# Target attention on one core: the small projections of the TensorE loop moved from inside the context to between turning and scores

## The reference

```
q = (target_item @ W_q).reshape(b, 4, 32)
k = (history @ W_k).reshape(b, 200, 4, 32)
v = (history @ W_v).reshape(b, 200, 4, 32)
scores = einsum('bhd,bshd->bhs', q, k) / sqrt(32)
scores = where(mask[:, None, :] == 0, -1e9, scores)
attn = softmax(scores, axis=-1)
y = einsum('bhs,bshd->bhd', attn, v).reshape(b, 128) @ W_o
```

## Time and profile before

| what | value |
|---|---|
| median of 3 runs | 581.31 us (579.66 to 874.48) |
| the profiled execution's own time | 575.58 us |
| its span, first to last instruction | 573.6 us |
| what lies around the span | 2.0 us |
| TensorE busy | 97% of the span |
| VectorE busy | 87% |
| packets of the main DMA queue | 96.4% of 16 engines' span |
| moved | 219.06 MB, 382 GB/s over the span |

### The profile page before, as it was taken

How to read it: one execution, slowest core, us unless ns; L and a number is a source line. 1 busy time by engine, 2 the same in 40 slices (tenths; PEclk the granted TensorE clock), 3 DMA queues, 4 the chain that set the end, 5 groups by cost and what they waited for, 6 DMA issues and landing times.

```text
span 573.6 us, 41769 instructions
## 1 busy us (share of the span) xinstructions
PE 553.6 (97%) x18612; PEld 444.7 (78%) x18612; DVE 497.4 (87%) x577; ACT 298.7 (52%) x949; POOL 307.3 (54%) x1126
## 2 busy tenths in 40 slices
PE   5878999999999999999999999999999999999996
PEld 5656878778887878787887888888788778878785
DVE  4876889999998988999998999989999899989970
ACT  2334555555455555555546555554655555455453
POOL 6844365565555556456546555655654555565500
PEclk9999999999999999999999999999999999999999
DMA  8998999999999999999999999999999999999940
GB/s 312 411 360 313 363 407 394 408 408 406 400 412 405 399 408 381 409 405 412 406 403 408 404 405 406 411 398 404 405 406 406 393 410 396 406 408 396 408 173 7
DMA packets 66120, 219.06 MB, mean 382 GB/s; under 512 B 7616, under 2 KB 16464, under 8 KB 66080
## 3 DMA queue, kind: packets, MB, share of 16 engines
q1 hardware_dynamic: 64800, 217.31, 96.4%
q0 software_dynamic: 704, 1.05, 0.5%
q10 hardware_dynamic: 576, 0.30, 0.2%
HBM read 217.58 MB, written 1.05 MB: 381 GB/s over the span
## 4 chain that ended last, share of the span: by engine, by line
PE 89%; DVE 3%; issue 3%; DMA 2%; SPq 1%; ACT 0%; POOLq 0%; POOL 0%; DVEq 0%
PE ps_c L288 35%; PE ps_s L258 31%; PE ps_p L271 10%; PE ps_y L298 6%; PE ps_u L243 4%; PE ps_u L305 4%; DVE blocks L477 3%; DMA hist<-r_history_sequence 2%; SPq L155 1%; ACT p_pad L412 0%; SPq L146 0%; DVE probs_t L498 0%; DVE neg_score L486 0%; POOLq L46 0%; POOL out L229 0%
## 5 line engine op out<-in xcount | busy, mean ns | idle before, releaser
L477 DVE STREAM_TRANSPOSE blocks<-hist 128x768 f32<-128x768 f32 (+2 forms) x320 | 469.8, 1490 | 51.8 <-DMA hist<-r_history_sequence 51.5
L201 POOL COPY u_pad<-u_sb 32x32 f32<-32x32 f32 x1024 | 234.4, 229 | 63.1 <-ACT u_sb L391 3.9
L288 PE MATMUL ps_c<-hist,p_pad 64*32 64x128 f32 x12800 | 217.4, 272 | 5.4 <-issue 4.6
L288 PEld LDWEIGHTS ps_c<-hist,p_pad 64*32 64x32 f32 x12800 | 182.6, 105 | 33.4 <-issue 25.3
L258 PE MATMUL ps_s<-blocks,u_pad 128*32 128x200 f32 x4096 | 189.1, 334 | 3.2 <-issue 1.9
L412 ACT ACTIVATE p_pad<-ps_p,own 128x200 f32<-128x200 f32 x512 | 170.2, 444 | 34.2 <-PE ps_p L271 34.2
L258 PEld LDWEIGHTS ps_s<-blocks,u_pad 128*32 128x32 f32 x4096 | 125.5, 110 | 46.6 <-DVE blocks L477 4.7
L205 POOL TENSOR_SCALAR bias<-mask 128x200 f32<-128x200 int32 x64 | 56.4, 882 | 175.9 <-DMA mask<-r_mask 175.7
L421 ACT COPY ctx_sb<-ps_c 128x128 f32<-128x128 f32 x128 | 27.8, 269 | 101.1 <-PE ps_c L288 101.1
L395 ACT ACTIVATE probs<-neg_score,neg_max 128x200 f32<-128x200 f32 x64 | 29.6, 463 | 95.5 <-DVE neg_max L486 95.5
L271 PE MATMUL ps_p<-probs_t,place_sel 128*64 128x112 f32 x1024 | 63.2, 265 | 1.2 <-DVE probs_t L498 0.9
(11 more groups left out here) (42 smaller groups left out, 83.1 us busy)
## 6 DMA issues: line engine op xcount, KB each, us to landing
hist<-r_history_sequence SPq DMA_DIRECT2D x128, 832.0 KB, 7.6
hist<-r_history_sequence SPq DMA_DIRECT2D x128, 512.0 KB, 6.0
hist<-r_history_sequence SPq DMA_DIRECT2D x128, 256.0 KB, 4.5
mask<-r_mask SPq DMA_DIRECT2D x64, 100.0 KB, 7.9
out<-out_sb POOLq DMA_DIRECT2D x21, 48.0 KB, 5.3
x_t<-r_target_item SPq DMA_DIRECT2D x1, 928.0 KB, 16.7
x_t<-r_target_item ACTq DMA_DIRECT2D x1, 96.0 KB, 4.4
w_in<-L_rec_W_k ACTq DMA_DIRECT2D x1, 64.0 KB, 1.9
```

What stands on the lines that cost most here:

```text
L201: pool.tensor_copy(to, source[Q * c:Q * c + Q, a]).then_inc(u_pad_ready, 1)
L288: mm = pe.matmul(ps_c[alpha][at:at + Q, 0:D], p_pad[rows, t + par, i, :], hist[2 * ring + i][rows, t + par, :], start=(t == 0), stop=(t + ...
L477: dve.transpose(blocks[g % BLOCKS][:, t0:t1].rearrange("p t c k -> p (t c k)"), hist[g % SLOTS][:, t0:t1, :].rearrange("p t d -> p (t d)") ...
```

## The change

Two things move. In TensorE's step, the small projection leaves the context, whose three pieces now follow each other, and stands between `turn_context` and `scores`. The kinds are dealt out anew: ring 0 does heads 2 and 3 of the next round, ring 1 does the outputs, ring 2 does heads 0 and 1 of the round after. The start does only heads 0 and 1 of round 1. On ScalarE the copy of the combined vectors and the copy of the output go to the end of the step's list, behind the copy of the turned context.

```diff
@@ step (TensorE)
                 turn_context()
+                if ring == 0:
+                    combine(r + 1, (2, 3))
+                if ring == 1:
+                    outputs(q - 1)
+                if ring == 2:
+                    combine(r + 2, (0, 1))
                 scores(q + 1, after, 0)
                 scores(q + 1, after, 1, q + 1)
-                for piece in range(len(PIECES) - 1):
+                for piece in range(len(PIECES)):
                     context(ring, piece)
-                if ring == 0:
-                    outputs(q)
-                else:
-
-                    combine(r + 2, (2 * ring - 2, 2 * ring - 1))
-                context(ring, len(PIECES) - 1)
...
-            combine(1, range(H))
+            combine(1, (0, 1))
@@ copy_combined (ScalarE)
-                act.wait_ge(u_done, r + 1 if r < 2 else 2 * r)
+                act.wait_ge(u_done, 2 * r + 1)
@@ the loop of ScalarE
                 exponent(q)
                 normalise(q)
+                if q >= 1:
+                    finish(q - 1)
+                expand(q)
+                if q >= 1:
+                    copy_context(q - 1)
                 r = q // RING
                 if q % RING == 0 and r + 1 < NR:
                     copy_combined(r + 1)
                 if q % RING == 1 and r >= 1:
                     store(r - 1)
-                if q >= 1:
-                    finish(q - 1)
-                expand(q)
-                if q >= 1:
-                    copy_context(q - 1)
```

## The result

The changed kernel is **slower**: 586.54 us median (585.75 to 588.28, 5 runs) against 581.31 (5 runs), a ratio of 1.0119 with a 95% interval of 1.0085 to 1.0152, so +5 to +9 us; the two medians alone differ by 5.2. The ratio is taken over fast runs, so without the one of 874.48 us that stands among the runs of before. The profiled execution took 585.75 us, its span 583.7. I had forecast 580.6: wrong in sign. The measured time lies outside the forecast's own range of 572.3 to 584.2, and inside the range of eight in ten (571 to 588) only because that one made room for rival B.

The account below looks back on a forecast made before the run. TensorE and the DMA engines were taken as both full, balanced to about 2%. Start +2.5, steady part -2.2 and end -1.0 gave -0.7 us, forecast as a 580.6 us median; own range 572.3 to 584.2, eight in ten 571 to 588.

Parts of the forecast that it names:

- rival B: Start: the new wait for the target transfer is paid in full, no earlier loss saved; 591 to 593 us; chance 0.12.
- The start's term: First iteration: combine's new wait for the large target transfer costs +2.5 us, between +0.4 and +3.9.
- The stop of the loads: Start: loads stop from 32 until slots come free at 37.8 and about 1 us more; 6.8 us lost.
- The wait itself: Ring 0, first iteration: TensorE idles about 10 us, from 22.4 until the target transfer lands at 32.8.
- The clock behind it: Combine and scores behind the start's wait: cold matmuls add 0 to 3.3 us, taken as 1.
- The steady part and the end: From 110 to 545 us -2.2 us, a quarter of 8.4; after the last load -1.0 us.
- GpSimd at no cost: GpSimd's spread begins later in one step of three, but its reader comes some 9 us later; cost 0.
- VectorE's longer wait for history: Steady part: TensorE's gain becomes waiting behind VectorE, whose wait for history grows beyond 51.5 us.
- Rival A: Steady part: TensorE is the real bound and loads speed up to 412 to 420 GB/s; 571.4 to 566.4 us; chance 0.13.
- Rival C: Context's break costs nothing or its gain comes back, loads gain nothing; only the start's +1 to +4 remains; chance 0.15.
- half-way case: Start: the wait for the target transfer is paid in part, +5 us, 586 us.
- far end: Start: wait of 11.4 us plus 1 to 3.3 for cold matmuls, less 3 elsewhere: +9.4 to +11.7, 591 to 593 us.

Follow-up runs that it names:

- e2: Kernel before, nothing moved, but TensorE waits for the large target transfer in ring 0 ahead of the scores; ratio 1.0168 to the kernel before.
- e1: Changed kernel, but ring 0's combine doesn't wait for the large target transfer in the first iteration; 578.25 us, ratio 0.9951 to the kernel before.
- e7: Kernel before with the outputs doing one head of four, so less TensorE work; ratio 0.9943 to the kernel before.
- e14: Kernel before with each mask from pair 3 on loaded a second time into a tile nobody reads; ratio 1.0220 to the kernel before.
- e9: Kernel before with the masks of pairs 3 to 63 not loaded; ratio 1.0123 to the kernel before.
- e8: Changed kernel with 116 transposes instead of 16 ahead of the loop, to keep TensorE busy until the wait; 585.53 us, ratio 1.0086 to the kernel before.

## Why the prediction was wrong

- **The start's term was mis-sized, and it decided the sign.** I took +2.5 us, between 0.4 and 3.9; e2 measured 9.8 (6.6 to 12.8). The step that failed is "some of that was lost anyway": I credited the 6.4 us of load time that the start loses before against the new loss. They don't overlap. They are lost for the most part in steps 1 and 2 (4.7 us, at 317 GB/s), *behind* the wait, and those took 21.96 us as they had taken 21.92. A delay ahead of a lossy stretch adds to it. Without the credit the same sum gives 6.8 to 10.3 us, which holds the measured one.
- **The stop of the loads was mis-sized too.** I had the first slots free at 37.8 and context 0 through at 40.2; it was 40.74 and 44.68. Of those last 4.5 us, 1.5 lie in the wait, 1.3 in combine and scores, and 1.7 in the context, whose wait on issue (1.30) came again. With the first slots free 2.9 us later than I had them, the 6.8 us become 9.7, next to the 9.8 measured without any credit.
- **The wait itself** was seen in place, cause and nearly in length: 11.97 us where I took about 10. Combine began at 34.28, where I had taken 32.8 for the landing: the transfer's last packets came from 32 us on at 37 GB/s and less.
- **The clock behind it** was left at 1 us of a range of 0 to 3.3. The rows give 0.52 (combine, 1.16 against 0.64) and 1.75 (scores, 4.66 against 2.91), 2.3 us. The rule of the Trainium skill that I had set beside it, with half speed for both and 3.3 us, was nearer, if not by much.
- **The steady part and the end** were right in their sum. I had -2.2 and -1.0, together -3.2; e1 against before measures -2.9 (-1.2 to -4.4). How it splits is not shown: from place of step 60 to the end the profile of e1 takes 38.02 us against 38.39 and 38.45 in the two of before, so the end gave 0.4 rather than 1.0. TensorE's own busy time fell by 0.19 us a step (8.40 to 8.21), just under my 0.22 to 0.32. That this turns into about 10 us of gaps is shown (10.5), and that they lie at place and scores.
- **GpSimd at no cost** was right: its wait for the combined vectors grew from 3.9 to 53.3 us, and TensorE never waits for it in the changed kernel's profile.
- **VectorE's longer wait for history** was wrong: 49.3 us and, in e1, 53.4, where the two profiles of before have 51.5 and 54.5. Its own work and the rate are the same, so its wait is; the gaps are TensorE's.
- **Rival A** is refuted by e7 and e14, and by the changed kernel itself: TensorE has gaps and the loads stay at 405 GB/s, where A needed 412 to 420.
- **Rival C** is refuted in its first half: the break's cost is gone from TensorE's step. Its second, that the loads gain nothing, can't be told from the profiles (8.40 us a step in e1 against 8.41 and 8.45), but e1's gain speaks against it, and the start cost more than its +1 to +4.
- **Rival B**, with 0.12 of the chance, is what happened: the start's wait is paid and no earlier loss is saved. In size it came out at its half-way case (+5 us, 586), not at its far end, since the start cost 9.8 us and not 12.4 to 14.7. Its ground, that "a stop of theirs is never made up", holds here: the changed kernel is 9.93 us behind e1 at step 3 and 10.8 at the end of the span.

What stays open: why leaving out masks or rows goes with slow packets, and so whether a kernel with fewer bytes could run at TensorE's step; and what the waits on issue in the first three steps are.

## What to carry to other kernels

When work with a wait is moved earlier in a loop, look at the first iteration: which data does it touch there, when does that land, and which releases stand behind the wait. Where the load engines are full, as here, a stretch in which they run dry goes into the end (9.8 us of it did), and losses that the start already has further on are no credit against it. A loop variable as an address can demand a wait that the first iteration's data doesn't need; taking it out turned +1.2% into -0.5%.

## What the runs showed of the hardware that was not expected

- Fewer bytes ran slower: without the masks, 3% of the bytes, a step of the order before went from 8.41 to 8.65 us and the loads from 404 to 381 GB/s (e9); with the masks doubled it went to 8.70 at 403 GB/s (e14).
- TensorE's granted clock was 0.50 from 36 to 38 us in e8, behind an idle time of 1.72 us, although 116 transposes had kept it busy, at 1.00, until place; from 34 to 35 us, at work again, it still had 1.00.
